# Graph edge matrix of a four-layer GNN: plain window scatters with pad columns in place of accumulating stream scatters

## What is computed

```python
h = relu(layernorm(x)); x = x + gcn(h)        # three rounds of segment_sum((z@W)[src] * norm, dst), relu
h = relu(layernorm(x)); x = x + gin(h)        # h + segment_sum(edge_weight * h[src], dst), two dense layers
h = relu(layernorm(x)); x = x + attention(h)  # 8 heads, softmax over the edges of one dst, three kinds of score
h = relu(layernorm(x)); x = x + sage(h)       # mean of h[src] over dst, dense, rows normalised
```

## Time and profile before

| | |
|---|---|
| median of 3 executions | 5555.98 us (5548.86 to 5559.23) |
| the profiled execution | 5525.34 us, its span 5523.6 us |
| TensorE busy | 4056.4 us (73%), mean granted clock 0.876 |
| GpSimd busy | 3418.5 us (62%) |
| VectorE busy | 1733.6 us (31%) |
| ScalarE busy | 1091.5 us (20%) |
| weights scatter, first to last start | 109.5 to 1783.2 us |
| counts scatter, first to last start | 2058.9 to 3707.4 us |

### The profile page before, as it was taken

How to read it: one execution, slowest core, us unless ns; L and a number is a source line. 1 busy time by engine, 2 the same in 40 slices (tenths; PEclk the granted TensorE clock), 3 DMA queues, 4 the chain that set the end, 5 groups by cost and what they waited for, 6 DMA issues and landing times.

```text
span 5523.6 us, 54861 instructions
## 1 busy us (share of the span) xinstructions
PE 4056.4 (73%) x17476; PEld 2188.9 (40%) x17476; DVE 1733.6 (31%) x4330; ACT 1091.5 (20%) x2843; POOL 3418.5 (62%) x2459
## 2 busy tenths in 40 slices
PE   4502113046370879999999999988999999949999
PEld 4402001012120335444444444435666666645444
DVE  7907000000000002000111100118999999970001
ACT  0002000000000000000000000017878888750000
POOL 1777777876658807777777777677777777520000
PEclk9755556578685889999999999999999999969999
DMA  9997446279692998999999999966777767608886
GB/s 313 357 354 206 103 84 167 20 228 331 209 350 19 418 387 274 314 305 303 311 310 308 308 292 289 293 203 151 155 155 155 152 154 153 135 22 317 302 304 244
DMA packets 714947, 1305.38 MB, mean 236 GB/s; under 512 B 276925, under 2 KB 478186, under 8 KB 659350
## 3 DMA queue, kind: packets, MB, share of 16 engines
q1 hardware_dynamic: 440195, 1222.92, 63.8%
q0 software_dynamic: 252624, 58.23, 12.8%
q10 hardware_dynamic: 21843, 20.72, 1.3%
HBM read 977.62 MB, written 326.38 MB: 236 GB/s over the span
## 4 chain that ended last, share of the span: by engine, by line
PE 53%; DMA 18%; POOL 13%; DVE 8%; issue 6%; SPq 1%; DVEq 0%; ACT 0%; POOLq 0%; ACTq 0%
PE psum L1056 38%; DMA graph<-ew_col,work 14%; POOL graph L845 12%; DMA pool<-graph 4%; PE psum L1326 3%; PE psum L1302 2%; PE psum L1284 2%; PE psum L1291 2%; DVE work L2384 1%; PE psum L1277 1%; PE psum L1269 1%; DVE pool L2059 1%; DVE pool L2319 1%; PE psum L1314 1%; DVE pool L2317 1%
## 5 line engine op out<-in xcount | busy, mean ns | idle before, releaser
L1056 PE MATMUL psum<-pool,work 128*128 128x512 f32 (+2 forms) x6370 | 2700.1, 583 | 919.1 <-DMA pool<-graph 918.0
L1056 PEld LDWEIGHTS psum<-pool,work 128*128 128x128 f32 (+1 forms) x6370 | 1192.0, 196 | 2364.5 <-issue 1959.8
L845 POOL DMA_INDIRECT graph<-work x782 | 1208.6, 1546 | 571.7 <-DMA graph<-work 248.1
L845 POOL DMA_INDIRECT graph<-ew_col,work x782 | 1215.0, 1554 | 547.2 <-DMA graph<-ew_col,work 240.3
L898 POOL DMA_INDIRECT gath<-table,src_col x520 | 508.5, 978 | 182.5 <-issue 138.4
L1537 ACT ACTIVATE QV<-QV,col_bias 128x512 f32<-128x512 f32 (+1 forms) x39 | 27.1, 696 | 2413.0 <-DVE QV L1851 2413.0
L1816 DVE COPY QV<-psum 128x512 f32<-128x512 f32 (+1 forms) x13 | 8.6, 661 | 1515.9 <-PE psum L1056 1515.9
L898 POOL DMA_INDIRECT ew_col<-table,src_col x312 | 300.8, 964 | 95.1 <-issue 94.2
L1827 DVE TENSOR_TENSOR QV<-QV,psum 128x512 f32<-128x512 f32 x48 | 33.0, 688 | 927.6 <-PE psum L1056 927.6
L1326 PEld LDWEIGHTS psum<-pool,hot 128*128 128x128 f32 x1664 | 208.7, 197 | 253.5 <-issue 247.9
L1326 PE MATMUL psum<-pool,hot 128*128 128x72 f32 x1664 | 236.3, 284 | 79.6 <-DVE work L2384 76.0
(11 more groups left out here) (321 smaller groups left out, 3570.4 us busy)
## 6 DMA issues: line engine op xcount, KB each, us to landing
pool<-graph SPq DMA_DIRECT2D x425, 1792.0 KB, 7.1
graph<-zeros SPq DMA_DIRECT2D x85, 1792.0 KB, 21.6
graph<-zeros SPq DMA_DIRECT2D x24, 4096.0 KB, 24.9
pool<-edge_attr SPq DMA_DIRECT2D x832, 64.0 KB
pool<-step_masks SPq DMA_DIRECT2D x624, 48.0 KB
pool<-rel_rows SPq DMA_DIRECT2D x208, 128.0 KB
graph<-ew_col,work POOLq DMA_INDIRECT x782
graph<-work POOLq DMA_INDIRECT x782
```

The costliest lines, as they stand in the source:

```text
L845: gp.indirect_dma_start(out=graph[which][:, :], out_offset=bass.IndirectOffsetOnAxis(ap=place[:, t:t + 1], axis=0), in_=values[:, t:t + 1] ...
L1056: ins = pe.matmul(psum[:, bank, 0:w], source[0:n, b, :], ring[0:n, m % RING, (b - lo) * w:(b - lo + 1) * w], start=(b == 0), stop=(b == NB ...
```

## The change

A window is now four tiles (`WIN`), 196 in all. Each tile's keys are compared with those of all four tiles of its window, so that every pair's sum over the whole window is made in PSUM by four matmuls per tile, and only its first edge writes it. A node that goes on from one window to the next gets its later part in one of 195 pad columns behind the edge panel, which becomes 304 columns wide. So no element of the matrix is written twice, and the scatter drops `compute_op`; GpSimd waits only for the window four back. An edge from a node to itself gets one added in the sum (`loop_col`), since the write replaces the identity. The comparisons are one VectorE instruction per tile of the window; a share for ScalarE is in the code but `on_scalar` returns False. Zeros for 55 of the 89 pieces of the counts matrix are written before pass 0. The step-row gathers move from behind chunk 0 to behind window 88, the gather of the distances from behind chunk 0 to behind window 32 of the counts. `add_pads` sums runs of pads with a scan and adds all 195 without waits in between; the closing of the edge panel in passes 1 to 4 moves from the next panel to block 4 of the one after.

```diff
+    WIN = 4
+    NWIN = ceil_div(NT, WIN)
+    PADS = NWIN - 1
+    WIDTH = [BANK] * EDGE_PANEL + [ceil_div(PAD_AT + PADS, 16) * 16]
     TURN = 8
+    BATCH = WIN * TURN
...
+        STEPS_AT = 88
+        ATT_AT = 32
+        FIRST_AT = 4
+        EARLY_ZEROS = PER_PASS * 5 // 8
...
             zero_weights()
+            for m in range(EARLY_ZEROS):
+                write_zeros(*zeros_of(*all_pieces[m]))
...
-                    if nth == 0:
-                        zero_counts(p, lo, hi)
+                    if nth == 0 and m >= EARLY_ZEROS:
+                        sp.dma_start(*zeros_of(*all_pieces[m])).then_inc(counts_zeroed, 16)
...
-                        if done[q]:
-                            gp.wait_ge(stream_done[q], 16 * done[q])
-                        gp.indirect_dma_start(
-                            out=graph[which][:, :], out_offset=bass.IndirectOffsetOnAxis(ap=place[:, t:t + 1], axis=0),
-                            in_=values[:, t:t + 1], in_offset=None, compute_op=ALU.add).then_inc(stream_done[q], 16)
...
+            def scatter(which, k, values):
+                if which == WEIGHTS and k % TURN == 0:
...
+                    gp.wait_ge(zeroed, zero_to[k // TURN % 5])
+                    gp.sem_inc(chunk_ready, 1)
+                    gp.wait_ge(placed, k // TURN + 1)
+                if k >= 4:
+                    gp.wait_ge(window_done[k % 4], window_value(which, k - 4))
+                    gp.sem_inc(built, 1)
+                for t in window_tiles(k):
+                    gp.indirect_dma_start(
+                        out=graph[which][:, :], out_offset=bass.IndirectOffsetOnAxis(ap=place[:, t:t + 1], axis=0),
+                        in_=values[:, t:t + 1], in_offset=None).then_inc(window_done[k % 4], 16)
...
+            for k in range(STEPS_AT):
+                scatter(WEIGHTS, k, ew_col)
             gp.wait_ge(steps_placed, PLACED_TILES)
...
-                    ins = pe.matmul(psum[:, 4 + b % 2, lo:lo + 5], equal[:, g % EQUALS, j, :], edge_parts[:, t + j, :], start=True,
-                                    stop=True)
+                    for i in range(WIN):
+                        n = VALUES if i <= j else VALUES - 1
+                        kind = OWN_TILE if i == j else LATER_TILE
+                        ins = pe.matmul(psum[:, 4 + b % 2, lo:lo + n], equal[:, k % EQUALS, i, j * P:(j + 1) * P],
+                                        edge_parts[:, k * WIN + i, kind, 0:n], start=(i == 0), stop=(i == WIN - 1))
...
-            if i >= 1 and b == CLOSE_AT:
+            if i == 2 and b == FIRST_AT:
+                gcn_close(pe, 1, 0, "W2")
+            if i >= 2 and b == CLOSE_AT:
                 gcn_close(pe, 1, i - 1, "W2")
...
+            v.tensor_tensor_scan(pad_runs, same_run, pads, 0.0, ALU.mult, ALU.add).then_inc(own.up(), 1)
+            settle()
+            STEP = 15
+            for first in range(0, PADS, STEP):
+                places = load_plan(mybir.EngineType.DVE, LIST_ROW, L_TARGET + first, min(STEP, PADS - first), NB * D + PADS - 1,
+                                   "places are numbers of nodes or of pads")
+                for k in range(min(STEP, PADS - first)):
+                    s = first + k
+                    node = OT[:, bass.ds(places[k], 1)]
+                    ins = v.tensor_tensor(node, node, pad_runs[:, s:s + 1], ALU.add)
+            ins.then_inc(pads_added, 1)
+            v.wait_ge(pads_added, nth + 1)
...
-                v.tensor_tensor(equal[:, g % EQUALS, :, :], psum[:, g % EQUALS, :].rearrange("p (j e) -> p j e", e=P),
-                                spread(key_col[:, t:t + GROUP].rearrange("p (j a) -> p j a", a=1), 2, P),
-                                ALU.is_equal).then_inc(equal_made, 1)
+                    for i in range(WIN):
+                        t = k * WIN + i
+                        ins = v.tensor_scalar(equal[:, k % EQUALS, i, :], psum[:, k % 4, :], key_col[:, t:t + 1], None, ALU.is_equal)
+                    ins.then_inc(equal_vector, 1)
```

More of the change, by code:

```diff
@@ L853, in gpsimd, with scattered @@
+            def scattered(which):
+                for k in range(NWIN - 4, NWIN):
+                    gp.wait_ge(window_done[k % 4], window_value(which, k))
+                    gp.sem_inc(built, 1)
+            zero_to = []
             gp.wait_ge(lists_made, 2)
-            zero_to = load_counts(mybir.EngineType.Pool, L_ZERO, NCH, PANELS)
-            gp.wait_ge(zeroed, zero_to[0])
-            gp.sem_inc(chunk_ready, 1)
-            scatter(WEIGHTS, 0, ew_col)
+            for k in range(STEPS_AT):
+                scatter(WEIGHTS, k, ew_col)
@@ L1831, in add_pads @@
+                v.wait_ge(sums_read, nth * PANELS + 1)
+                add_pads(v, own, settle, nth)
+            else:
+                here = OT[:, p * BANK:p * BANK + OWN[p]]
+                v.wait_ge(pieces_used, panel_done(nth, i))
+                v.tensor_tensor(here, here, psum[:, panel_bank(nth, i), 0:OWN[p]], ALU.add).then_inc(sums_read, 1)
+        def add_pads(v, own, settle, nth):
             v.wait_ge(sums_read, PANELS)
-            for first in range(0, PADS, PADS // 2):
-                nodes = load_plan(mybir.EngineType.DVE, LIST_ROW, L_BOUND + first, PADS // 2, N - 1, "bounds are numbers of nodes")
-                for k in range(PADS // 2):
-                    s = first + k + 1
-                    node = OT[:, bass.ds(nodes[k], 1)]
-                    settle()
-                    ins = v.tensor_tensor(node, node, OT[:, PAD + s:PAD + s + 1], ALU.add)
-                    if done is not None and s == PADS:
-                        ins.then_inc(done, 1)
-                        break
-                    ins.then_inc(own.up(), 1)
@@ L1914, in edges_vector @@
             step(v.tensor_scalar(row_base, part_no[:, :], float(NB), float(EDGE_PANEL * ROWS_OF), ALU.mult, ALU.add))
-            for q in range(STREAMS):
-                step(v.memset(trash_of[:, q, :], float(P + q)))
+            step(v.tensor_scalar(last_row, part_no[:, :], float(P - 1), None, ALU.is_equal))
+            step(v.tensor_scalar(trash_of, iota_f[:, 0:BATCH], float(WIDTH[EDGE_PANEL]), None, ALU.add))
+            step(v.tensor_copy(places, iota_f[:, :]))
             step(v.memset(flat(lead_rows), 1.0))
-            step(v.memset(flat(low_rows)[:, 0:1], 0.0))
@@ new lines, in lists_vector @@
+                row = slice(LIST_ROW, LIST_ROW + 1)
+                bound, slot, target = (list_f[:, k, 0:PADS] for k in range(3))
+                to, need = (need_f[row, k * PANELS:(k + 1) * PANELS] for k in range(2))
+                first = list_f[:, 1, 0:NWIN]
+                step(v.tensor_copy(first, lists[:, L_FIRST:L_FIRST + NWIN]))
+                step(v.tensor_scalar(to, iota_f[row, 0:PANELS], 1.0, float(BANK), ALU.add, ALU.mult))
+                settle()
+                step(v.tensor_tensor(needed, spread(first.rearrange("a (p w) -> a p w", p=1), 1, PANELS),
+                                     spread(to.rearrange("a (p w) -> a p w", w=1), 2, NWIN), ALU.is_lt))
@@ new lines, in lists_vector @@
+                settle()
+                step(v.tensor_reduce(need, needed, AX.X, ALU.add))
+                for lo in range(0, PADS, P):
+                    n = min(P, PADS - lo)
+                    step(v.tensor_scalar(slot[:, lo:lo + n], iota_f[row, 0:n], float(NB * D + lo), None, ALU.add))
+                step(v.memset(target[:, PADS - 1:PADS], 1.0))
+                step(v.tensor_tensor(target[:, 0:PADS - 1], bound[:, 0:PADS - 1], bound[:, 1:PADS], ALU.not_equal))
+                settle()
```

575 lines of the change are left out of this document (319 added, 256 removed).

## The result

The changed kernel takes **5087.3 us** (median of 4, 5085.4 to 5088.7), the kernel before beside it 5552.4: a ratio of 0.916, 95% interval 0.9145 to 0.9177. The prediction was 5099 us. Its profiled execution has a span of 5083.6 us, 440 shorter than that of before (5523.6). Four later sets of runs took longer for the kernel before too (5764 to 5783 us), and in the one of them that ran the changed kernel it was 24% *slower* than the one before (7200 us). Half of the experiments are about that. What differed between these sets and the first ones is not known.

What follows compares the result with a forecast made beforehand. GpSimd's scatters, 2.14 us a tile, bound the build with pass 0, matmuls the other passes. -637 + 53 + 74 + 8 + 43 + 6 - 4 = -457 gave 5068, 5099 by the median; 8 in 10: 4985 to 5370.

Steps and rivals of the forecast that it cites:

- Scatter, 1.28 us a tile: Edge-matrix build: GpSimd issues a plain scatter in 0.98 us plus 0.30 before the next; bounds 1.24 and 1.85.
- Rival 1: Issue cost belongs to any scatter, not the accumulate: 1.85 us a tile stays, 5358 us; chance 0.18.
- Comparisons at 0.61 us, end at 596: VectorE before pass 0: 784 comparisons of 128x512 plus 25 batches of 1.7, together 521 us from about 75.
- Landing to first matmul, 144 us: Before pass 0: from landed step-row gathers to the first matmul, 136 + 8 us, so pass 0 starts at 789.
- Zeros done by 760: DMA before pass 0: 55 of 89 pieces of counts zeros, 101 MB at 352 GB/s, written by about 760 us.
- Pass 0 of 634 us: Pass 0 from 789 to 1423: eight panels at 43 us, four at 63, edge panel 38; end moves by -637.
- Pads, 64 us: VectorE closing the edge panel: 13 loads 34 us, adds 27, with scan and waits 64; +53 after pass 0.
- Stalls of 20.5, 20.5, 19.5 and 13.5, restarts of 2 each: TensorE waiting for the closed edge panel in passes 1, 2, 3 and last: +74, restarts +8.
- Width, 14.3 us a pass and 6 in pass 1: Edge panel of 304 columns instead of 128: +43 in passes 2 to 4, +6 in pass 1.
- Counts scatter free: Second scatter, beside passes 1 to 3: off the path, DMA cost taken as 0, +77 us kept for the range.
- Attention, -4: Between pass 3 and the last pass: the memset no longer waits for the counts scatter, -4 us.
- Rival 4: Slower than before: plain 4-byte writes load the DMA engines and starve panel loads; 5871 at 0.9 us a scatter; chance 0.03.

Runs made afterwards that it cites:

- accumulate: Changed kernel with the scatters accumulating again (`compute_op` put back), all else the same: 5324.2 us, ratio 0.960, early set.
- one_comparison: Changed kernel with the four comparisons of a window made one instruction of 128x2048: 5072.8 us, ratio 0.915, early set.
- aligned_loads: Changed kernel with pad register loads of 16 places instead of 15, so each begins at a multiple of four words: 4989.9 us, ratio 0.900, early.
- no_pad_adds: Changed kernel without the loads of places and the 195 pad adds, edge panel still wide: 4953.3 us, ratio 0.893, early set.
- paced_short: Changed kernel plus loads of 16, one comparison per window, 44 early zero pieces, and an unread 4-column GpSimd power after each window: 5259.6 us, 0.912, late.

## Why the prediction was right, and where not

The time was right because the main steps were, in the conditions in which the trace of before was taken. That the median came out within 12 us is in part luck, as the last point says. By its own terms:

- **Scatter, 1.28 us a tile:** right, 1.26; the accumulate is what costs the other 0.59 (accumulate). Rival 1 named exactly what was shown to be false.
- **Comparisons at 0.61 us, end at 596:** mis-sized. They take 0.66 each, 2.64 a window, and end at 639: 43 us late, and GpSimd waited 116 us before the step-row gathers where 71 stood. The row of 896 columns in 1.14 us had been taken as a rate per column; an instruction of 512 columns takes 0.74. The upper bound of the term was 0.69. This is the largest error of the sum.
- **Landing to first matmul, 144 us:** right, 144.5. Pass 0 started at 835.5 instead of 789, the 43 and a few us of the plan.
- **Zeros done by 760:** 780.6. Not on the path yet, and next in line behind the comparisons, as one_comparison showed: of 86 us that VectorE gained, 14 arrived.
- **Pass 0 of 634 us:** 619, with eight panels at 44 us and 268 us for the five others, where 290 stood. This hides 15 us of the late start. Together pass 0 ends 605 us sooner, not 637.
- **Pads, 64 us:** right in sum (62.3) and in parts: loads leave VectorE idle 1.5 to 2.0 and 3.4 us (1.6 and 3.1 taken), adds at 0.12 (0.14). The gap after pass 0 grew by 47, not 53: the pads took 51.6 more, and the first matmul of pass 1 now comes 7 us after the last add instead of 12.
- **Stalls of 20.5, 20.5, 19.5 and 13.5, restarts of 2 each:** 18.0, 18.3, 17.5 and 12.6; with the restarts, 20 to 21 and 15 by aligned_loads. Right, and shown to be the pads' by no_pad_adds.
- **Width, 14.3 us a pass and 6 in pass 1:** right, 14 to 15 and 7.
- **Counts scatter free:** right in the early runs; passes 1 to 3 show only width and stalls. In the late ones it was not: pass 1 grew by 758 us.
- **Attention, -4:** -8.6.
- Sum: -440 where -457 stood, from profile to profile. The forecast of 5099 also kept the 30.6 us by which the profiled execution of before lies under its median. That gap was not there after (5085.4 against 5087.3). The sum was 17 us too hopeful and this term 29 too dear, so that the median came out 12 under the forecast.

**Rival 4** was a loss by the DMA engines, from 0.70 us of DMA time a scatter. A loss exists in the late runs, by another path: the share of the DMA engines is 0.35 in pass 1 while TensorE is held up. The trace of before does not show it: its scatters are 1.55 us long and broken by waits, and it was taken early. The chance of 0.03 for slower was too small for a change that makes one engine issue 782 transfers without a rest for the first time; the prediction had looked at bytes and engines alone.

## What to carry to other kernels

Price an indirect DMA by whether it accumulates: here 0.96 us of GpSimd against 1.55. Summing in PSUM first bought that, and it let more scatters be in flight. When values are read into registers, let each load begin at a multiple of four words: one number, 15 to 16, gave 97 us. And when an engine is freed to issue transfers back to back, measure on several occasions and chips, with the old kernel beside the new one each time, and try a short pause in the loop: 1 us in 6 went with 1820 us less where it mattered. What it costs in the early conditions was not measured. The best version found early is aligned_loads (0.900), late paced_short (0.912); paced_short was not tried early, nor aligned_loads late.

## What the runs showed of the hardware that was not expected

- Two sets of runs, about an hour apart, gave the same kernel 5087 and 7200 us, and the kernel before 5552 and 5783. A chip numbered 7 gave the kernel before 5542 us in one set and 5773 in another.
- In the late runs, scatters at 1.26 to 1.40 us without a break slowed TensorE to one record in 2.8 us and VectorE's 195 small adds from 59.5 to 186 us. The slow pace lasted 28 and 25 us beyond the last scatter of the two.
- A register load of 16 words that begins at a multiple of four words leaves VectorE idle 1.09 us, one of 15 words 1.54 us if it begins there and 3.43 us if not. The Trainium skill, "Runtime: NRT & Kernel Launch", section "Instruction fetch mechanics", gives about 200 ns a register, and its page means registers loaded from HBM; these loads are from SBUF, and the idle time is 0.07, 0.10 and 0.23 us a register.
- One comparison of 128x2048 with both operands as tensors takes 2.28 us (eight in 17.7, 2.21 from one to the next); four of 128x512 with one scalar a row take 2.64 from window to window, for the same elements from the same PSUM bank.
- The granted clock of TensorE was 0.50 from 100 to 600 us in the changed kernel, with TensorE busy half the time, and 0.94 in the comparisons of before. VectorE bounds that stretch, so it cost nothing.
